# Squares of the gated result on ScalarE instead of GpSimd, with the steps of all engines in a new order

## What is computed

```python
def mamba2(x, Win, conv_w, conv_b, dt_bias, A_log, D, gnorm, Wout):
    z, xBC, dt = split(x @ Win)                    # 128, 160, 8 columns
    xBC = silu(conv_b + sum(xp[:, k:k + l, :] * conv_w[k] for k in range(4)))
    xs, B, C = split(xBC)                          # 128, 16, 16
    dt = softplus(dt + dt_bias); dA = exp(dt * -exp(A_log))
    h = dA_t * h + xdt_t * B_t                     # scan over the sequence, 8 heads
    y = (h . C_t + D * xs) * silu(z)
    return rmsnorm(y, gnorm) @ Wout                # x * rsqrt(mean(x * x) + eps) * w
```

## Time and profile before

| what | value |
|---|---|
| median of 3 runs | 1256.41 us (1254.06 to 1258.2) |
| the profiled execution | 1250.45 us, its span 1248.5 us |
| mean granted clock of TensorE | 0.966 |
| busy share of the span, PE / DVE / ACT / POOL | 88% / 67% / 61% / 25% |
| main loop, 24 blocks | about 60 to 980 us of the span |
| norm, routing and experts | the rest, from about 980 us |

### The profile page before, as it was taken

The page is one execution under the profiler, slowest core; times in us unless marked ns, Lnnn a source line. Parts: engine busy times, 40 slices in busy tenths (PEclk is TensorE's granted clock), DMA queues, the critical chain, the costliest instruction groups (busy, mean ns, idle before and its releaser), DMA issues.

```text
span 1248.5 us, 46550 instructions
## 1 busy us (share of the span) xinstructions
PE 1094.0 (88%) x20216; PEld 568.9 (46%) x20216; DVE 836.2 (67%) x1219; ACT 756.2 (61%) x1450; POOL 312.1 (25%) x306
## 2 busy tenths in 40 slices
PE   2699989999999999989989999998987339999998
PEld 1355555555555545555454555555544223333332
DVE  4378666787666876668766687666876565656564
ACT  2477777677777677767777767776765113333332
POOL 7422232332223223232232322323222400000000
PEclk9799999999999999999999999999999558999999
DMA  4100110201111011110111101111000500000000
GB/s 84 23 18 7 30 30 19 44 5 31 31 31 33 2 31 31 31 32 4 30 31 31 33 2 31 31 31 33 9 7 14 85 1 1 1 9 9 1 9 9
DMA packets 66354, 28.75 MB, mean 23 GB/s; under 512 B 53416, under 2 KB 61928, under 8 KB 66152
## 3 DMA queue, kind: packets, MB, share of 16 engines
q1 hardware_dynamic: 66152, 25.78, 9.7%
HBM read 9.96 MB, written 1.05 MB: 9 GB/s over the span
## 4 chain that ended last, share of the span: by engine, by line
PE 72%; DVE 11%; issue 8%; ACT 6%; POOL 1%; DMA 1%; SPq 0%; ACTq 0%; DVEq 0%; POOLq 0%
PE ring L681 14%; PE ybank L766 10%; PE ring L893 6%; DVE em L1275 5%; PE ybank L908 5%; PE ring L746 5%; PE ring L899 4%; PE oss L778 4%; PE ring L705 4%; PE ring L691 4%; PE oss L781 3%; PE ring L633 2%; PE xtb L735 2%; PE ring L723 2%; ACT rstd L971 1%
## 5 line engine op out<-in xcount | busy, mean ns | idle before, releaser
L1275 DVE TENSOR_TENSOR em<-em,gs 128x1536 f32<-128x1536 f32 (+1 forms) x192 | 296.4, 1565 | 8.4 <-ACT em L1004 7.8
L1004 ACT ACTIVATE em<-ring 128x512 f32<-128x512 f32 x480 | 248.4, 597 | 9.5 <-PE ring L746 5.5
L766 PE MATMUL ybank<-em,xdt 64*32 64x64 f32 (+1 forms) x12288 | 186.7, 238 | 26.3 <-issue 19.5
L566 POOL TENSOR_TENSOR ysq<-yg 128x512 f32<-128x512 f32 x96 | 130.6, 1360 | 282.9 <-DVE yg L1295 282.9
L766 PEld LDWEIGHTS ybank<-em,xdt 64*32 64x32 f32 x12288 | 154.1, 106 | 83.9 <-issue 55.2
L746 PE MATMUL ring<-rt,lt 128*64 128x512 bf16 x960 | 144.9, 393 | 9.7 <-ACT em L1004 6.1
L1148 ACT ACTIVATE em<-ring 128x512 f32<-128x512 f32 x128 | 69.5, 595 | 137.4 <-PE ring L893 137.4
L1303 DVE TENSOR_TENSOR on<-oss,rr 128x256 f32<-128x256 f32 x96 | 40.6, 423 | 150.5 <-ACT rr L1014 150.5
L1446 DVE TENSOR_TENSOR em<-em,ring 128x512 f32<-128x512 f32 x128 | 82.2, 684 | 83.6 <-PE ring L899 81.3
L1012 ACT ACTIVATE rr<-oss,eps 128x256 f32<-128x256 f32 x96 | 45.5, 474 | 112.1 <-PE oss L781 111.9
L1282 DVE SCALAR_TENSOR_TENSOR yt<-xs,col,ybank 128x256 f32<-128x256 f32 x192 | 83.1, 473 | 35.5 <-PE ybank L766 35.3
(11 more groups left out here) (166 smaller groups left out, 1514.0 us busy)
## 6 DMA issues: line engine op xcount, KB each, us to landing
x_b<-x_t SPq DMA_DIRECT2D x48, 128.0 KB, 3.0
cm<-bc SPq DMA_DIRECT2D x24, 224.0 KB, 2.7
rt<-lt SPq DMA_DIRECT2D x120, 24.0 KB
cw<-in_L_conv_t_cw SPq DMA_DIRECT2D x6, 320.0 KB, 3.3
cw<-in_L_conv_b_cw SPq DMA_DIRECT2D x6, 320.0 KB, 3.1
x_in<-in_x SPq DMA_DIRECT2D x4, 256.0 KB, 4.4
xs<-in_L_ffn_w SPq DMA_DIRECT2D x2, 512.0 KB, 7.0
zs<-in_L_ffn_w SPq DMA_DIRECT2D x2, 512.0 KB, 9.1
```

Source lines behind the costliest of these rows:

```text
L566: pool.tensor_tensor(out=ysq[c % 2][:], in0=yg[c % 2][:], in1=yg[c % 2][:], op=ALU.mult).then_inc(s_ysq, 1)
L766: mm = pe.matmul(ybank[QUAD * q:QUAD * (q + 1), ab, to:to + hi - lo], xdt[m % 2][rows, 8 * (i % 2) + 4 * first + q, r, :], em[rows, p % EM ...
L1004: emptied(act.activation(em[:, p % EM_SLOTS, :, HALF * j:HALF * (j + 1)], o.rearrange("p (h t) -> p h t", h=HEADS), ACT.Exp), "seg", n, i, ...
L1275: dve.tensor_tensor(e, e, gs[n % 2][:, i:i + 1, 0:wide].to_broadcast([P, HEADS, wide]), ALU.mult).then_inc(s_w, 1)
```

## The change

- `square_y` leaves POOL and becomes an ACTIVATE with the function Square on ACT, of the same size (128 x 512), between the same semaphores. POOL is left with `add_x` and the preparation of weights.
- The lists of PE, ACT and DVE are written in a new order, and `ring_turns` with them. No step is added or dropped.
- `s_cross` is split into one semaphore per batch, with the same events behind it.

```diff
-            def square_y(k, c):
-                m = 4 * k + c
-                pool.wait_ge(s_yg, m + 1)
-                if m >= 2:
-                    pool.wait_ge(s_o, m - 1)
-                pool.tensor_tensor(out=ysq[c % 2][:], in0=yg[c % 2][:], in1=yg[c % 2][:], op=ALU.mult
-                                   ).then_inc(s_ysq, 1)
...
+            def square_y(k, c):
+                m = 4 * k + c
+                act.wait_ge(s_yg, m + 1)
+                if m >= 2:
+                    act.wait_ge(s_o, m - 1)
+                act.activation(ysq[c % 2][:], yg[c % 2][:], ACT.Square).then_inc(s_ysq, 1)
...
@@ -1084,32 +1078,38 @@
                 if k:
+                    square_y(k - 1, 3)
+                exps(k, 2)
+                if k:
                     inverse_root(k - 1, 3)
-                exps(k, 2)
                 exps(k, 3)
...
@@ -1326,41 +1327,41 @@
                 weigh(k, 0)
+                weigh(k, 1)
                 x_dt(k, 1)
                 if k:
                     norm_out(k - 1, 3)
-                weigh(k, 1)
                 weigh(k, 2)
...
@@ -115,14 +115,14 @@
         t.two("x", n, 1)
         t.one("cum", n)
+        t.two("z", n, 0)
         t.two("bc", n)
         t.one("parts", n)
-        t.two("z", n, 0)
         t.two("z", n, 1)
```

More of the change, by code:

```diff
@@ L231, in build @@
         s_cm = sem("c_rows_placed")
-        s_cross = sem("residual_crossed")
+        s_cross = [sem(f"residual{u}_crossed") for u in range(2)]
         s_rt = sem("target_rows_placed")
@@ L806, in _ @@
                 more = n < NBLOCK
+                decays(k, 2)
                 turn_x(k, 1)
@@ L809, in _ @@
                     project_out(k - 1, 3)
-                decays(k, 2)
+                decays(k, 3)
                 mix_states(k, 0)
-                decays(k, 3)
+                mix_states(k, 1)
+                decays(k, 4)
                 turn_x(k, 2)
-                decays(k, 4)
-                mix_states(k, 1)
                 if more:
                     mean(n, 1)
+                mix_states(k, 2)
                 decays(k, 5)
-                mix_states(k, 2)
                 mix_states(k, 3)
+                project_out(k, 0)
                 if more:
@@ L824, in _ @@
                 turn_x(k, 3)
-                if more:
-                    turn_dt(n)
-                project_out(k, 0)
                 decays(k, 7)
@@ L830, in _ @@
                 if more:
+                    turn_dt(n)
                     project_x(n, 0)
@@ L837, in _ @@
                 if more:
+                    project_z(n, 0)
                     project_bc(n)
                     turn_parts(n)
-                    project_z(n, 0)
                     project_z(n, 1)
+                mix_states(k, 6)
                 project_out(k, 2)
-                mix_states(k, 6)
                 if more:
                     gram(n)
-                mix_states(k, 7)
+                    turn_x(n, 0)
                 if n + 1 < NBLOCK:
                     mean(n + 1, 0)
+                mix_states(k, 7)
                 if more:
-                    turn_x(n, 0)
                     decays(n, 0)
@@ L1094, in _ @@
                     rstd_of(n, 1)
+                square_y(k, 0)
                 exps(k, 5)
@@ L1098, in _ @@
                 exps(k, 6)
-                inverse_root(k, 0)
                 exps(k, 7)
+                square_y(k, 1)
                 if more:
                     softplus(n)
+                inverse_root(k, 0)
                 inverse_root(k, 1)
@@ L1106, in _ @@
                     silu_x(n, 0)
-                    silu_x(n, 1)
-                    silu_bc(n)
                 if n + 1 < NBLOCK:
@@ L1111, in _ @@
                 if more:
+                    silu_x(n, 1)
                     silu_z(n, 0)
+                    silu_bc(n)
+                square_y(k, 2)
+                if more:
                     silu_z(n, 1)
@@ L1335, in _ @@
                 weigh(k, 3)
+                gate_y(k, 0)
                 if more:
                     h_of(n, 1)
-                gate_y(k, 0)
                 x_dt(k, 2)
+                weigh(k, 4)
                 add_skip(k, 1)
-                weigh(k, 4)
+                gate_y(k, 1)
                 if more:
                     bias_dt(n)
+                weigh(k, 5)
                 norm_out(k, 0)
-                gate_y(k, 1)
-                x_dt(k, 3)
-                weigh(k, 5)
                 if more:
                     finish_dt(n)
+                norm_out(k, 1)
                 weigh(k, 6)
-                weigh(k, 7)
-                norm_out(k, 1)
+                x_dt(k, 3)
                 if more:
@@ L1358, in _ @@
                     rows_of_cum(n)
+                weigh(k, 7)
+                if more:
+                    x_dt(n, 0)
                 norm_out(k, 2)
@@ L1361, in _ @@
                 gate_y(k, 3)
-                if more:
-                    x_dt(n, 0)
             norm_out(NBLOCK - 1, 3)
```

11 lines of the change are left out of this document (4 added, 7 removed).

## The result

The changed kernel takes **1265.7 us** (median of 7 runs, 1263.84 to 1270.23) beside 1258.2 us for the kernel before in the same session (7 runs, 1254.06 to 1261.97): ratio 1.0069, 95% interval 1.0047 to 1.0091. The prediction was 1264.7 us, slower. The profiled execution is the one of 1265.7 us, with 1264.0 of it in the span.

The account below looks back on a forecast made before the run. PE, busiest at 88%, was taken as the bound, gains lying in its waits. 1250.45 us profiled + 32.9 for the new order - 24.6 for fewer "issue" waits = 1258.8, with 6.0 to the median: 1264.7 us, range 1242 to 1287.

Parts of the forecast that it names:

- Part 1: Squares taken off POOL: no gain, since POOL sat idle before them and `project_x` covers the held-up `finish_dt`.
- Part 2: Squares on ACT: 0.64 us each, 61 us in all, 2.6 us a block, on an engine with a quarter free.
- Part 3: Start of a block, `decays(k, 2)` ahead of `turn_x` and `project_out`: +1.2 us a block.
- the walk: Hand timing of old and new orders through four blocks; gave +1.43 us a block for the new, untested there.
- Part 4: `inverse_root(k - 1, 3)` behind a square and three exps, so `mean(n, 1)` waits for the residual: +0.6 us a block.
- Part 5: Copy of C's rows before `gram`: 0.3 us to spare left, a wait of 0.1 to 0.3 us.
- Part 6: "Issue" waits at neighbouring dense PE steps, short of instructions; spreading them credits 1.07 us a block, -24.6 us.
- Rival A: No relief, "issue" waits not bound to neighbouring steps: 1289.3 us, chance 0.13.
- Rival B: Faster: all "issue" waits go, and `add_x(k - 1, 3)` gets in ahead of `weigh(k, 2)`: 1244.7 us, chance 0.27.
- C's first form: A draw: all "issue" waits go, the late-residual wait stays: 1253.2 us; chance 0.15 for the draw in either form.

Follow-up runs that it names:

- The best order: New order of all four engines, found by a search with a model, all squares on GpSimd as in the kernel before: 1229.82 us, ratio 0.9755.
- the mixed order: Against the kernel before, square 1 alone on ScalarE, the others on GpSimd, with a new model-found order on all four engines: 1251.31 us, ratio 0.9924.
- both runs on it: Kernel before with PE's dense steps spread out: 1268.75 us; changed kernel with its dense steps closed up at one place: 1289.98 us.

## Why the prediction was right, and where it was not

**The sum: right by luck.** The prediction is 1250.45 us, plus 8.3 for the new order, plus 6.0 because the median of the kernel before lay that far above its profiled execution. Between the two profiled executions, with the clock granted alike, the change costs 15.3 us, nearly twice the 8.3: 0.70 us a block where 0.36 was forecast. And the 6.0 did not come at all, since the profiled execution of the changed kernel is the median of its runs: as far as the clocks of the runs and the profile of the run with 64 empty instructions show it, that offset is clock that the kernel before loses and the changed one keeps. An error of -7.0 and one of +6.0 cancel. Of the 0.70, the relief was larger than forecast (-1.24 for -1.07), and the waits on other engines were undersized (+1.94, the last three rows of the table, for +1.43), if all that grew in busy and unlisted time is counted as such.

**Part 1, squares off POOL: right.** `finish_dt` fell to 0.28 us and nothing came of it. It takes 0.30 us in the run with the new order and the squares on POOL too, so what held it in the old order was a square beside it, not that POOL has the squares. The best order says it with more force: PE waits 3.9 us in 808 for POOL's squares there.

**Part 2, the price of a square: right** (0.641 us x 96 = 61.6 forecast as 61). **Its place: wrong.** "Squares 3 (of the block before) and 0 stand between exps that PE waits for, and are charged in part 3": so the prediction books ACT's added work under the order. The run with the squares alone shows 48.7 us of PE waits on the squares with the old order.

**Part 3, the start of a block: size about right, cause wrong.** Forecast were 1.2 us a block: "New order: `decays(k, 2)` stands ahead of both". The rows are `decays` 11.8 (over 15 was expected, 5.6 before), `project_out` 5.0 (5 to 14), and 0.64 us a block in busy time, less than half of it shown in `decays`. But putting `decays` back costs 1.7 us a block more. The failed step is that the walk was read as a difference of old and new, move by move, while the old order with the squares on ACT was never walked. The corrected walk gives that order +49 us (expectation of the mixed order, above), and `decays(k, 2)` would have stood there as its remedy. The price of 1.7 us a block for the old place holds the lower clock too, 0.45 of it at most.

**Part 4, the late residual: right in size and mechanism** (15.5 us in 18 waits, up to 1.0; forecast 10 to 17), down to the sum on POOL that is held for 2.17 us. That it is a cost of where `inverse_root` stands is wrong in the same way as part 3: the other place costs 11 us more by the medians, and 1.8 us more by the one execution that was profiled.

**Part 5, C's rows: wrong, small.** 0.1 to 0.3 us a block of `gram` waiting on the copy was forecast; no such row is in the trace.

**Part 6, the "issue" waits: right in the main.** 10.2 us were left, 17 forecast; both runs on it went the way of its reading, if less far in "issue" waits than expected. The credit was too small because of `mix_states(k, 1)`, which it counted in full: the stops in or right behind it are two, 1.1 us in all. `gram` was given half and keeps more (5.9 us of 8.3), `mix_states(k, 3)` about a third (3.0 of 8.5). "A `mix_states` that stands alone has none" has an exception in the trace of before, 0.40 us at 376.67 inside one that follows a `decays`. Rival A (no relief) fell, though the regular spacing that it went by is real in the count of instructions. The Trainium skill's "mostly hidden" (the same section) holds here by number: 96 of 134 places show no stop. By time the 38 others are 36.3 us in 808, up to 2.3 us at once, and the sum that the prediction took from it, no credit, does not hold: 26 us of them went with the order. Rival B needed all of the stops gone; 10.2 us remained. So did C's first form.

## What to carry to other kernels

An engine with a quarter of its time free can be full in the one stretch where the critical engine listens to it: price moved work by what is queued at the moment it becomes ready, not by shares. When a change moves work and reorders to suit, run both halves alone and cost the fourth corner too (here +3.3%, +3.2%, +0.7% together), or the remedy is booked as the disease. Before trusting a move, give the old placement an order sought in the same way: here that order was worth 2.4% by the medians (1.6% at one clock), and no order found with the move came near it. And before adding a median's distance from a profiled execution to a forecast, look at the granted clock of both: that distance may belong to the old kernel alone.

## What was not expected of the hardware

PE's stops without a wait came at every 256th instruction of its queue or not at all (249 stops in twelve traces, all within three places of one another in the count), and how long they last depends on what stands before them: the same 20216 matmuls have 36.3, 29.0, 23.6, 21.3, 15.3, 10.2 or 6.5 us of them in 808, in different orders. The granted clock is a part of what an order costs: 17 us at the lower level made the same kernel 0.34 us a block slower, with the same waits, and twelve of the sixteen falls in that run and in the one with `decays` put back came right behind a wait of 1.5 to 2.1 us. And a run of matmuls in the trace can hold a microsecond of waits with no idle time shown (ten in 2.36 us where eight take 1.16), so that two kernels here whose listed waits are alike, 41.0 and 42.0 us, differ by 21 us in time; the count of instructions in a window of fixed length tells them apart.
